# Taking both pairs of expert tiles of a step together in a fused attention and expert kernel

## The chip, the cores and the metric

The kernel runs on one core of one Trainium2 chip. The metric is the device time of one launch in microseconds; less is better. The engines are TensorE (PE; PEld is its weight load), VectorE (DVE), ScalarE (ACT), GpSimd (POOL) and SyncE (SP). SP, and here also POOL, issue DMAs in the order of their programs; a wait in such a queue holds up everything behind it.

## The reference

For 4096 token rows (two sequences of 2048, 256 features), the result is the input plus two branches over its layer norm: a linear attention of 16 heads in blocks, and an expert feed-forward of 64 routed experts (four per token, width 64) and two shared ones.

```python
xn = _layernorm(x, axis=-1)
x = x + attn(xn, slope_rate, w_qkv, w_gate, w_out, norm_w) + ffn(xn, ...)

# attn, by blocks of one head
o_inter = einsum('bhmd,bhde->bhme', qi * q_decay, kv)
qk = einsum('bhmd,bhnd->bhmn', qi, ki) * diag_decay
o_intra = einsum('bhmn,bhne->bhme', qk, vi)
kv_new = block_decay * kv + einsum('bhmd,bhme->bhde', ki * k_decay, vi)

# ffn
g = silu(einsum('nd,edf->nef', flat, wg))
u = einsum('nd,edf->nef', flat, wu)
routed = einsum('ne,nef,efd->nd', comb, g * u, wd)
```

`comb` holds the weights of the four experts that each token chose; all other entries are zero.

## The kernel before

A first phase computes the layer norm, the shared experts and the routing. A long second phase is a software pipeline of 128 steps (`NSTEP`), one for each head (16) and each group of 512 tokens (8): a step projects keys and values (`project_kv`), q and the gate for its group, and finishes the attention of the group before: key/value products (`keys_values`), scores (`scores`), attention (`attend`) and two halves of the output projection (`project_out`). Every eighth step begins a new head. The next head's weights come through the buffer `raw` in five parts, one a step (`load_head`); the last is the decay table (L389), which is issued at the end of the SP program of step s with s % 8 = 1. VectorE opens step s % 8 = 2 with `scale_out` (L891), which waits for all of them.

The routed experts ride along in steps 27 to 74 (`EXPERT0`, `EXPERT1`). The tokens' rows have been scattered to 192 tiles of 128 slots, each of which belongs to one expert; two tiles are a pair, 96 pairs in all, two pairs a step. The way of a pair q, with buffers by q % 2 unless said otherwise:

- SP loads its rows to `xs` (`load_rows`, L413). VectorE turns them by blocks of 32 into the one buffer `xz` (`turn_rows`, L1063). POOL stores `xz` to HBM and reads it back in four pieces as `xsT` (L573, L578), the transposed rows.
- SP reads the expert's number of each tile from the table `etab` into a register and issues the load of its gate and up weights (`we`, L419) and of its down weights (`wd`, L420): `load_experts`, two tiles a pair. It is called by `pair_done(q)`, behind the wait for the down matmuls of pair q, for the pair q + 2. `pair_done` then waits for the results and stores them (L437).
- TensorE multiplies gate and up (`gate_up`, L1306) into bank 7, ScalarE takes the silu (`silu_pair`, L709), VectorE the product of both (`gated`, L1068), the hidden products `hT`. TensorE multiplies them by the down weights (`down`, L1314) into banks 6 and 7, and ScalarE copies the result to `ys` (`result`, L715).

The order of each engine is written out by hand in a loop over the steps at the end of its program. In an expert step the first pair's gate/up matmuls stand before the output projection, its down matmuls behind the q projection; the scores follow, then the second pair's gate/up matmuls, `attend`, the second half of the output projection, the gate projection and the second pair's down matmuls. The table read of SP is this:

```python
e = sp.value_load(etab[0:1, bass.ds(q * 2 + j, 1)], min_val=0, max_val=E - 1)
sp.dma_start(we[r][:, j, :], at(wexp, e)).then_inc(pair_loaded[r], 16)
sp.dma_start(wd[r][j * F:(j + 1) * F, :], at(wdown, e)).then_inc(pair_loaded[r], 16)
```

SP's other work in a step: the turned keys are stored (`store_keys`, L399, behind VectorE's turning, L1029) and read back in four pieces (`load_keys`, L405), the rows of later pairs are loaded, and a part of a head's weights.

Of the kernel before, what the change touches and what calls it, by code (L numbers as in the profile page):

```python
# [8 lines left out]
I32 = mybir.dt.int32  # L9
U32 = mybir.dt.uint32  # L10
ALU = mybir.AluOpType
# [46 lines left out]
def lightning_moe(nc, x, slope, wqkv, wgate, wout, norm_w, router_w, router_bias,  # L58
# [11 lines left out]
    with top:  # L70
# [15 lines left out]
        etab = keep("etab", [1, 2 * P], I32)  # L86
# [24 lines left out]
        sg = keep("sg", [P, 2 * P])  # L111
        hT = keep("hT", [P, P])
        ys = [keep(f"ys{i}", [P, 2, D]) for i in range(2)]
        with ExitStack() as st:
            lc = sb_in(st)("lc", [P, NT, E])
        with ExitStack() as st:
            sb = sb_in(st)
            xz = sb("xz", [P, BLK, 2 * KD, TB])
            xsT = [sb(f"xsT{i}", [P, BLK, 2 * KD, TB]) for i in range(2)]
# [160 lines left out]
        xz_stored = sem("xz_stored")  # L280
# [14 lines left out]
        pair_loaded = many("pair_loaded", 2)  # L295
# [48 lines left out]
        def _(sp):  # L344
# [116 lines left out]
            for s in range(SLOTS + 1):  # L461
                q0 = 2 * (s - EXPERT0)
                experts = EXPERT0 <= s < EXPERT1
                if EXPERT0 < s <= EXPERT1:
                    pair_done(q0 - 1)
# [14 lines left out]
                if EXPERT0 - 1 <= s < EXPERT1:  # L480
                    load_rows(q0 + 5)
# [18 lines left out]
        def _(pool):  # L500
# [920 lines left out]
```

## Time and profile before

| | us |
|---|---|
| median of 3 runs | 1780.21 (1774.66 to 1787.95) |
| span of the profiled execution, first to last instruction | 1777.0 |
| TensorE busy in the span | 1718.2 (97%) |
| VectorE busy | 1308.8 (74%) |
| ScalarE busy | 718.8 (40%) |
| POOL busy | 605.1 (34%) |

The profiled execution is known by its span, which lies between the shortest and the longest of the timed runs, 3.2 us below their median. Matmul records overlap in a pipeline, so a busy TensorE is not TensorE at its peak. The time that SP spends on issuing is not counted as busy; it is read from the SP queue in order of time, and from its waits. A profile names for each idle stretch of an engine what ended it.

### The profile page before, as it was taken

How to read it: one execution, taken by the hardware profiler on the slowest of the kernel's cores; microseconds unless marked ns; L12 is line 12 of the kernel's file. 1: busy time of each engine (PE TensorE's matmuls, PEld its weight loads, DVE VectorE, ACT ScalarE, POOL GpSimd, SP SyncE). 2: the span in 40 equal slices, each digit the busy share in tenths (PEclk: the TensorE clock that was granted, in tenths of full speed). 3: DMA queues.
4: the chain of work that ended last, by engine and by line, in shares of the span. 5: the costliest groups of instructions: out<-in, count | busy, mean ns of one | idle time of the engine just before them, and what ended most of it. 6: DMA issues, size and time to landing. Idle time of an engine off the chain costs nothing.

```text
span 1777.0 us, 34485 instructions
## 1 busy us (share of the span) xinstructions
PE 1718.2 (97%) x11705; PEld 1520.5 (86%) x11705; DVE 1308.8 (74%) x2590; ACT 718.8 (40%) x1331; POOL 605.1 (34%) x826
## 2 busy tenths in 40 slices
PE   6999999999899999999999999999999999999997
PEld 5888899999788888887888888889898989899996
DVE  7888788888576666666766666668787877876666
ACT  4333343443344444444444444443334343434331
POOL 2223155655343334333333433323232424200011
PEclk9999999999999999999999999999999999999998
DMA  6666444444478888787888888844343434331234
GB/s 216 214 219 229 140 140 137 140 148 140 152 218 252 246 252 244 219 257 235 250 250 245 250 242 240 255 150 134 104 134 105 141 110 142 110 93 49 78 101 131
DMA packets 283502, 316.02 MB, mean 178 GB/s; under 512 B 37696, under 2 KB 233280, under 8 KB 283328
## 3 DMA queue, kind: packets, MB, share of 16 engines
q1 hardware_dynamic: 237120, 200.52, 36.9%
q0 software_dynamic: 33792, 88.13, 16.8%
q10 hardware_dynamic: 12416, 25.17, 3.8%
q8 instruction: 96, 1.57, 0.4%
q14 instruction: 78, 0.64, 0.1%
HBM read 169.21 MB, written 144.46 MB: 177 GB/s over the span
## 4 chain that ended last, share of the span: by engine, by line
PE 81%; DVE 7%; DMA 4%; issue 3%; SPq 3%; ACT 1%; POOL 0%; DVEq 0%; ACTq 0%
PE bank L1241 7%; PE bank L1283 6%; PE bank L1242 6%; PE bank L1243 6%; PE bank L1266 6%; PE bank L1223 6%; PE bank L1221 6%; PE bank L1222 6%; PE bank L1286 6%; PE bank L1274 5%; PE bank L1306 4%; PE bank L1314 3%; PE bank L1295 3%; PE bank L1297 3%; PE bank L1296 3%
## 5 line engine op out<-in xcount | busy, mean ns | idle before, releaser
L578 POOL DMA_DIRECT2D xsT<-rows_turned x384 | 210.7, 555 | 366.6 <-DMA rows_turned<-xz 346.8
L1241 PE MATMUL bank<-wh,xh 128*128 128x256 f32 x1024 | 293.8, 287 | 0.0
L1243 PE MATMUL bank<-wh,xl 128*128 128x256 f32 x1024 | 289.1, 282 | 0.0
L1242 PE MATMUL bank<-wl,xh 128*128 128x256 f32 x1024 | 289.0, 282 | 0.0
L674 ACT ACTIVATE kv<-bank 128x512 f32<-128x512 f32 x256 | 153.1, 598 | 229.3 <-PE bank L1243 229.3
L589 POOL DMA_INDIRECT yk<-slot_y,pos x128 | 130.5, 1020 | 270.9 <-DVE xr L995 183.6
L1283 PE MATMUL bank<-sm,kv 128*128 128x128 f32 x1024 | 201.2, 284 | 14.6 <-DVE sm L1009 14.5
L1241 PEld LDWEIGHTS bank<-wh,xh 128*128 128x128 f32 x1024 | 193.3, 189 | 19.2 <-issue 15.9
L1221 PE MATMUL bank<-xh,wh 128*128 128x512 f32 x512 | 208.9, 408 | 0.0
L1045 DVE SCALAR_TENSOR_TENSOR og<-tg,bank 128x512 f32<-128x512 f32 x128 | 88.0, 688 | 157.7 <-ACT o L700 157.7
L1223 PE MATMUL bank<-xh,wl 128*128 128x512 f32 x512 | 202.4, 395 | 0.0
L1029 DVE STREAM_TRANSPOSE kz<-kv 128x512 f32<-128x512 f32 x127 | 90.1, 710 | 151.8 <-issue 139.1
L1222 PE MATMUL bank<-xl,wh 128*128 128x512 f32 x512 | 201.8, 394 | 0.0
L1242 PEld LDWEIGHTS bank<-wl,xh 128*128 128x128 f32 x1024 | 192.6, 188 | 3.1
L1243 PEld LDWEIGHTS bank<-wh,xl 128*128 128x128 f32 x1024 | 192.9, 188 | 0.0
L1286 PE MATMUL bank<-qp,state 128*128 128x128 f32 x960 | 187.9, 278 | 0.0
L1283 PEld LDWEIGHTS bank<-sm,kv 128*128 128x128 f32 x1024 | 159.5, 194 | 30.1 <-DVE sm L1009 20.6
L681 ACT ACTIVATE qT<-bank 128x512 f32<-128x512 f32 x128 | 76.5, 597 | 234.1 <-PE bank L1223 208.5
L1058 DVE TENSOR_TENSOR acc<-acc,bank 128x512 f32<-128x512 f32 x240 | 163.6, 682 | 4.3 <-PE bank L1297 2.7
L1023 DVE SCALAR_TENSOR_TENSOR state<-state,hc,bank 128x128 f32<-128x128 f32 x448 | 152.1, 339 | 15.0 <-PE bank L1274 2.4
L700 ACT ACTIVATE o<-bank 128x512 f32<-128x512 f32 x128 | 76.7, 599 | 188.7 <-PE bank L1286 187.6
L1266 PEld LDWEIGHTS bank<-qT,kT 128*128 128x128 f32 x1024 | 129.4, 192 | 27.0 <-issue 21.6
(165 smaller groups left out, 3699.0 us busy)
## 6 DMA issues: line engine op xcount, KB each, us to landing
keys_turned<-kz SPq DMA_DIRECT2D x127, 256.0 KB, 2.9
kT_by_group<-keys_turned SPq DMA_DIRECT2D x508, 64.0 KB
slot_x<-zeros ACTq DMA_DIRECT2D x8, 3072.0 KB, 9.9
we<-wexp_in SPq DMA_DIRECT2D x192, 128.0 KB, 2.8
xs<-slot_x SPq DMA_DIRECT2D x96, 256.0 KB, 4.3
rows_turned<-xz POOLq DMA_DIRECT2D x96, 256.0 KB, 3.9
xsT<-rows_turned POOLq DMA_DIRECT2D x384, 64.0 KB, 3.2
slot_y<-ys SPq DMA_DIRECT2D x96, 256.0 KB, 2.8
```

Of the source, the lines that this page charges most:

```text
L578: pool.dma_start(xsT[q % 2][b * TB:(b + 1) * TB, :, :, :].rearrange("p a k j -> p a (k j)"), xz_back[q % 2, b]).then_inc(xsT_loaded[q % 2] ...
L674: act.activation(kv[i % 2][:, 2 * half:2 * half + 2, :].rearrange("p c n -> p (c n)"), bank[half][:], ACT.Silu).then_inc((k_silu, v_silu)[ ...
L1058: dve.tensor_tensor(a, a, bank[5][:], ALU.add).then_inc(acc_added, 1)
L1221: pe.matmul(dst, lh, rh, start=(k == 0), stop=False)
L1222: pe.matmul(dst, lh, rl, start=False, stop=False)
L1223: mm = pe.matmul(dst, ll, rh, start=False, stop=(k == KD - 1))
L1241: pe.matmul(dst, lh, rh, start=(k == 0), stop=False)
L1242: pe.matmul(dst, lh, rl, start=False, stop=False)
L1243: mm = pe.matmul(dst, ll, rh, start=False, stop=(k == KD - 1))
L1266: mm = pe.matmul(bank[2][:, ch[c]], kT[:, c, :, :].rearrange("p a j -> p (a j)"), qT[:, ch[c]], start=True, stop=True)
L1283: mm = pe.matmul(bank[4][:, ch[c]], kv[j % 2][:, c, HD:2 * HD], sm[:, ch[c]], start=True, stop=empty)
L1286: mm = pe.matmul(bank[4][:, ch[c]], state[j % 2][:, c, :], qp[j % 2][:, ch[c]], start=False, stop=True)
```

## The change

Both pairs of a step (2u and 2u + 1, a quad u) are taken together. TensorE runs the gate/up matmuls of both pairs one behind the other into all 512 columns of bank 7, where the first pair's stood, and the down matmuls of both behind the q projection. There is one silu of 512 columns, two products of twice the size (written back over `sg`, and `hT` is gone), and two result copies of 512 columns. The scores come before the q projection in every step. There are two `xz` buffers, and VectorE turns the rows of both pairs of the next step at the head of the step. SP loads gate/up weights of the next quad behind the wait for this quad's gate/up matmuls, and down weights behind the wait for its down matmuls, with a function for each; both read the expert's number from the table.

On SP, from the result store of a pair to the next, with `etab` the table, `we` the gate/up weights and `wd` the down weights; before, in the middle of an expert step:

```order
L437 DMA slot_y<-ys 128x2x256
L399 DMA keys_turned<-kz 128x512
L413 DMA xs<-slot_x 128x2x256
L418 TENSOR_LOAD etab
L418 ISA x2
L419 ISA
L419 DMA we<-wexp_in 128x256
L420 ISA
L420 DMA wd<-wdown_in 64x256
```

Now, at the last gate/up load and the first down load of a step:

```order
L420 TENSOR_LOAD etab
L420 ISA x2
L421 ISA
L421 DMA we<-wexp_in 128x256
L405 DMA kT_by_group<-keys_turned 32x4x128 x4
L428 TENSOR_LOAD etab
L428 ISA x2
L429 ISA
L429 DMA wd<-wdown_in 64x256
```

Where one table read served two loads, each load now has one of its own, and the four reads and loads of the down weights stand behind the key loads.

On TensorE, in an expert step from the end of the q projection on (`kT` and `qT` are of the scores, `sm` of `attend`); before:

```order
L1223 MATMUL bank<-xh,wl 128x512
L1314 MATMUL bank<-wd,hT 128x256 x2
L1266 MATMUL bank<-qT,kT 128x128 x4
L1306 MATMUL bank<-xsT,we 128x128 x4
L1283 MATMUL bank<-sm,kv 128x128
```

Now, from the scores on:

```order
L1277 MATMUL bank<-qT,kT 128x128 x4
L1232 MATMUL bank<-xh,wh 128x512
L1233 MATMUL bank<-xl,wh 128x512
L1234 MATMUL bank<-xh,wl 128x512
L1232 MATMUL bank<-xh,wh 128x512
L1233 MATMUL bank<-xl,wh 128x512
L1234 MATMUL bank<-xh,wl 128x512
L1329 MATMUL bank<-wd,sg 128x256 x4
L1294 MATMUL bank<-sm,kv 128x128
```

The scores moved ahead of the q projection, the second gate/up run went to the first one, and the one down run is twice as long.

The core of the diff:

```diff
...
                     sp.wait_ge(xz_ready, q - 1)
                 sp.dma_start(xs[q % 2][:], slot_x_pair[q]).then_inc(pair_rows_loaded[q % 2], 16)
 
-            def load_experts(q):
+            def load_gate_up(q):
+                if q >= NPAIR:
+                    return
                 r = q % 2
                 for j in range(2):
                     e = sp.value_load(etab[0:1, bass.ds(q * 2 + j, 1)], min_val=0, max_val=E - 1)
-                    sp.dma_start(we[r][:, j, :], at(wexp, e)).then_inc(pair_loaded[r], 16)
-                    sp.dma_start(wd[r][j * F:(j + 1) * F, :], at(wdown, e)).then_inc(pair_loaded[r], 16)
+                    sp.dma_start(we[r][:, j, :], at(wexp, e)).then_inc(we_loaded[r], 16)
+
+            def load_down(q):
+                if q >= NPAIR:
+                    return
+                r = q % 2
+                for j in range(2):
+                    e = sp.value_load(etab[0:1, bass.ds(q * 2 + j, 1)], min_val=0, max_val=E - 1)
+                    sp.dma_start(wd[r][j * F:(j + 1) * F, :], at(wdown, e)).then_inc(wd_loaded[r], 16)
 
             def first_pairs():
                 sp.wait_ge(routed, 1)
                 sp.wait_ge(wgt_ready, 1)
                 for q in range(2):
-                    load_experts(q)
+                    load_gate_up(q)
+                    load_down(q)
                 for r in range(CH):
                     sp.wait_ge(scattered[r], 16 * TOPK * NT // CH)
                 for q in range(2):
                     load_rows(q)
 
-            def pair_done(q):
-                sp.wait_ge(y_mm, q + 1)
-                if q + 2 < NPAIR:
-                    load_experts(q + 2)
-                sp.wait_ge(ys_ready, q + 1)
-                sp.dma_start(slot_y_pair[q], ys[q % 2][:]).then_inc(y_stored[q % 2], 16)
+            def next_gate_up(u):
+                sp.wait_ge(gu_mm, u + 1)
+                for r in range(2):
+                    load_gate_up(2 * u + 2 + r)
+
+            def quad_done(u):
+                sp.wait_ge(y_mm, u + 1)
+                for r in range(2):
+                    load_down(2 * u + 2 + r)
+                sp.wait_ge(ys_ready, u + 1)
+                for r in range(2):
+                    sp.dma_start(slot_y_pair[2 * u + r], ys[:, r, :, :]).then_inc(y_stored[r], 16)
 
             def load_part(t):
                 sp.wait_ge(part2_stored[t % 2], 16 * (t // 2))
...
                     store_part(COMBINE.index(s))
                 if EXPERT0 - 1 <= s < EXPERT1:
                     load_rows(q0 + 4)
+                    load_rows(q0 + 5)
                 if experts:
-                    pair_done(q0)
+                    next_gate_up(s - EXPERT0)
                 if 1 <= s < NSTEP:
                     load_keys(s)
                 if s == EXPERT0 - 2:
                     first_pairs()
-                if EXPERT0 - 1 <= s < EXPERT1:
-                    load_rows(q0 + 5)
+                if experts:
+                    quad_done(s - EXPERT0)
                 if s == EXPERT1:
                     for r in range(2):
                         sp.wait_ge(y_stored[r], 16 * NPAIR // 2)
...
                         pool.indirect_dma_start(out=slot_x, out_offset=bass.IndirectOffsetOnAxis(pos[:, q * CH + r, k:k + 1], 0),
                                                 in_=xs[r // 2][:, r % 2, :], in_offset=None).then_inc(scattered[r], 16)
 
-            for q in range(NPAIR):
-                pool.wait_ge(xz_ready, q + 1)
-                pool.wait_ge(xsT_loaded[q % 2], 16 * BLK * (q // 2))
-                pool.dma_start(xz_dram[q % 2], xz[:].rearrange("p b k j -> p b (k j)")).then_inc(xz_stored, 16)
-                pool.wait_ge(xz_stored, 16 * (q + 1))
-                if q >= 2:
-                    pool.wait_ge(gu_mm, q - 1)
-                for b in range(BLK):
-                    pool.dma_start(xsT[q % 2][b * TB:(b + 1) * TB, :, :, :].rearrange("p a k j -> p a (k j)"),
-                                   xz_back[q % 2, b]).then_inc(xsT_loaded[q % 2], 16)
+            for u in range(NPAIR // 2):
+                for r in range(2):
+                    pool.wait_ge(xz_ready, 2 * u + r + 1)
+                    pool.wait_ge(xsT_loaded[r], 16 * BLK * u)
+                    pool.dma_start(xz_dram[r], xz[r][:].rearrange("p b k j -> p b (k j)")).then_inc(xz_stored[r], 16)
+                if u > 0:
+                    pool.wait_ge(gu_mm, u)
+                for r in range(2):
+                    pool.wait_ge(xz_stored[r], 16 * (u + 1))
+                    for b in range(BLK):
+                        pool.dma_start(xsT[r][b * TB:(b + 1) * TB, :, :, :].rearrange("p a k j -> p a (k j)"),
+                                       xz_back[r, b]).then_inc(xsT_loaded[r], 16)
             for r in range(2):
                 pool.wait_ge(y_stored[r], 16 * NPAIR // 2)
             for t in range(NT):
...
                 act.wait_ge(out_mm, KD * j)
                 act.copy(ogh[:], og[:]).then_inc(ogh_ready, 1)
 
-            def silu_pair(q):
-                act.wait_ge(gu_mm, q + 1)
-                act.activation(sg[F:2 * F, :], bank[7][0:F, 0:2 * P], ACT.Silu).then_inc(sg_ready, 1)
-
-            def result(q):
-                act.wait_ge(y_mm, q + 1)
-                act.wait_ge(y_stored[q % 2], 16 * (q // 2))
+            def silu_quad(u):
+                act.wait_ge(gu_mm, u + 1)
+                act.activation(sg[F:2 * F, :, :, :].rearrange("p r j n -> p (r j n)"), bank[7][0:F, :],
+                               ACT.Silu).then_inc(sg_ready, 1)
+
+            def result(u):
+                act.wait_ge(y_mm, u + 1)
+                for r in range(2):
+                    act.wait_ge(y_stored[r], 16 * u)
                 for j in range(2):
-                    ins = act.copy(ys[q % 2][:, j, :], bank[6 + j][:, 0:D])
+                    ins = act.copy(ys[:, :, j, :], bank[6 + j][:].rearrange("p (r d) -> p r d", r=2))
                 ins.then_inc(ys_ready, 1)
 
             for s in range(NSTEP + 1):
                 experts = EXPERT0 <= s < EXPERT1
-                q0 = 2 * (s - EXPERT0)
                 projects, attends = s < NSTEP, 1 <= s
                 if projects:
                     silu_kv(s, 0)
                     silu_kv(s, 1)
-                if attends and not experts:
+                if attends:
                     copy_kT(s - 1)
                 if experts:
-                    silu_pair(q0)
+                    silu_quad(s - EXPERT0)
                 if s % NSB == 3 and s // NSB + 1 < NH:
                     if s < NSB:
                         first_phase_stored(act)
...
 
             def turn_rows(q):
                 dve.wait_ge(pair_rows_loaded[q % 2], 16 * (q // 2 + 1))
-                dve.wait_ge(xz_stored, 16 * q)
-                dve.transpose(xz[:], xs[q % 2][:].rearrange("p t (k b i) -> p b (t k) i", b=BLK, i=TB)).then_inc(xz_ready, 1)
-
-            def gated(q):
-                dve.wait_ge(sg_ready, q + 1)
+                dve.wait_ge(xz_stored[q % 2], 16 * (q // 2))
+                dve.transpose(xz[q % 2][:], xs[q % 2][:].rearrange("p t (k b i) -> p b (t k) i", b=BLK, i=TB)).then_inc(xz_ready, 1)
+
+            def gated(u):
+                dve.wait_ge(sg_ready, u + 1)
+                up = bank[7][F:2 * F, :].rearrange("p (r j n) -> p r j n", r=2, j=2)
                 for j in range(2):
-                    dve.tensor_tensor(hT[j * F:(j + 1) * F, :], sg[F:2 * F, j * P:(j + 1) * P],
-                                      bank[7][F:2 * F, j * P:(j + 1) * P], ALU.mult).then_inc(hT_ready, 1)
+                    dve.tensor_tensor(sg[j * F:(j + 1) * F, :, j, :], sg[F:2 * F, :, j, :], up[:, :, j, :],
+                                      ALU.mult).then_inc(hT_ready, 1)
 
             def mean_squares(b):
                 dve.wait_ge(rms_mm, b + 1)
...
                 if attends:
                     update_state(s - 1)
                 if experts:
-                    gated(q0)
-                if attends and not experts:
+                    if projects:
+                        decay_keys(s)
+                    gated(s - EXPERT0)
+                if attends:
                     decay_scores(s - 1)
-                if projects:
+                if projects and not experts:
                     decay_keys(s)
-                if EXPERT0 <= s + 1 < EXPERT1:
-                    turn_rows(q0 + 3)
                 if delivers:
                     add_out(s - 2, 0)
-                if experts:
-                    decay_scores(s - 1)
                 if projects:
                     decay_queries(s)
                 if s > FIRST_OUT + 2:
                     last_sum(s - FIRST_OUT - 3)
-                if experts:
-                    gated(q0 + 1)
                 if attends:
                     gate_o(s - 1)
                 if delivers:
...
                 pe.matmul(bank[5][:], lh, ogl[:], start=False, stop=False)
                 pe.matmul(bank[5][:], ll, ogh[:], start=False, stop=True).then_inc(out_mm, 1)
 
-            def gate_up(q):
+            def gate_up(u):
                 pe.wait_ge(routed, 1)
-                pe.wait_ge(pair_loaded[q % 2], 64 * (q // 2 + 1))
-                pe.wait_ge(xsT_loaded[q % 2], 16 * BLK * (q // 2 + 1))
-                pe.wait_ge(ys_ready, q)
-                for j in range(2):
-                    for k in range(KD):
-                        mm = pe.matmul(bank[7][:, j * P:(j + 1) * P], we[q % 2][:, j, k * P:(k + 1) * P],
-                                       xsT[q % 2][:, :, j * KD + k, :], start=(k == 0), stop=(k == KD - 1))
+                pe.wait_ge(ys_ready, u)
+                for r in range(2):
+                    pe.wait_ge(we_loaded[r], 32 * (u + 1))
+                    pe.wait_ge(xsT_loaded[r], 16 * BLK * (u + 1))
+                    for j in range(2):
+                        for k in range(KD):
+                            mm = pe.matmul(bank[7][:, (2 * r + j) * P:(2 * r + j + 1) * P], we[r][:, j, k * P:(k + 1) * P],
+                                           xsT[r][:, :, j * KD + k, :], start=(k == 0), stop=(k == KD - 1))
                 mm.then_inc(gu_mm, 1)
 
-            def down(q):
-                pe.wait_ge(hT_ready, 2 * (q + 1))
-                for j in range(2):
-                    ps = slice(j * F, (j + 1) * F)
-                    mm = pe.matmul(bank[6 + j][:, 0:D], hT[ps, :], wd[q % 2][ps, :], start=True, stop=True)
+            def down(u):
+                pe.wait_ge(hT_ready, 2 * (u + 1))
+                for r in range(2):
+                    pe.wait_ge(wd_loaded[r], 32 * (u + 1))
+                for r in range(2):
+                    for j in range(2):
+                        ps = slice(j * F, (j + 1) * F)
+                        mm = pe.matmul(bank[6 + j][:, r * D:(r + 1) * D], sg[ps, r, j, :], wd[r][ps, :], start=True, stop=True)
                 mm.then_inc(y_mm, 1)
 
             def total_counts():
...
```

## Rows read from the trace of the kernel before

**Rows 1.** The page's part 1: busy time, share of the span, instructions.

```profile
PE 1718.2 (97%) x11705; PEld 1520.5 (86%) x11705; DVE 1308.8 (74%) x2590; ACT 718.8 (40%) x1331; POOL 605.1 (34%) x826
```

**Rows 2.** Windows, steps 27 to 74, score matmuls (L1266) alone: busy (x records).

```profile
489.00:1178.00 689.00, 56.51 (x384) 47.27 (x384) 1.00 0.81 242
```

**Rows 3.** Same windows: us; PE, PEld, DVE, ACT, POOL busy; clock, DMA, GB/s.

```profile
489.00:1178.00 689.00, 678.89 (x4656) 577.66 (x4655) 463.25 (x924) 308.69 (x636) 259.84 (x473) 1.00 0.81 242
```

**Rows 4.** Longest of TensorE's waits in that stage: total us, times, longest.

```profile
PE bank L1314 <- DVE hT L1068: 9.5, 5, 3.0
```

**Rows 5.** Waits of the SP queue in that stage: total us, times, longest.

```profile
SPq L418 <- PE bank L1314: 45.6, 39, 2.2
SPq L399 <- DVE kz L1029: 12.4, 8, 7.8
SPq L413 <- DVE xz L1063: 4.8, 12, 0.8
SPq L436 <- ACT ys L715: 2.9, 1, 2.9
```

**Rows 6.** The SP queue in order of time, step 34: start us, us issuing.

```profile
589.50 0.36 SPq L419 DMA_DIRECT2D we<-wexp_in  x1
590.04 0.48 SPq L420 DMA_DIRECT2D wd<-wdown_in  x1
591.33 0.35 SPq L419 DMA_DIRECT2D we<-wexp_in  x1
...
597.03 0.49 SPq L420 DMA_DIRECT2D wd<-wdown_in  x1
598.97 0.36 SPq L419 DMA_DIRECT2D we<-wexp_in  x1
```

**Rows 7.** The SP queue in order of time, step 42.

```profile
702.55 0.47 SPq L389 DMA_DIRECT2D raw<-decay_tables  x1
...
709.00 0.33 SPq L399 DMA_DIRECT2D keys_turned<-kz  x1
```

**Rows 8.** VectorE in order of time, opening of step 42; idle before in brackets.

```profile
708.00 0.35 DVE L891 TENSOR_SCALAR wos<-raw 128x256 f32<-128x256 f32 x1 [5.57 <-DMA raw<-decay_tables]
708.26 0.70 DVE L1029 STREAM_TRANSPOSE kz<-kv 128x512 f32<-128x512 f32 x1
```

**Rows 9.** TensorE in order of time, first down run of step 32.

```profile
565.01 0.39 PE L1222 MATMUL bank<-xl,wh 128*128 128x512 f32 x1
565.24 0.40 PE L1223 MATMUL bank<-xh,wl 128*128 128x512 f32 x1
565.57 0.70 PE L1314 MATMUL bank<-wd,hT 64*128 64x256 f32 x4
566.20 1.16 PE L1266 MATMUL bank<-qT,kT 128*128 128x128 f32 x8
567.20 1.06 PE L1306 MATMUL bank<-xsT,we 128*128 128x128 f32 x8
568.14 0.49 PE L1283 MATMUL bank<-sm,kv 128*128 128x128 f32 x2
```

**Rows 10.** Source line 418, the table read: duration ns min/median/max.

```profile
L418 SPq TENSOR_LOAD <-etab x192: 262/273/1059, 467.7 to 1166.0; - x192
L418 SPq FUSED_REGOPS  x192: 152/156/177, 468.2 to 1166.2; - x192
L418 SPq SEQ_ASSERT  x192: 18/18/33, 468.4 to 1166.5; - x192
```

**Rows 11.** Line 389, the decay-table load: who waited (us, times); landing.

```profile
  DVE wos L891: 32.3, 12
DMA to landing us min/median/max: 2.2/3.1/5.4
```

**Rows 12.** Windows around VectorE's wait in step 42; columns as in rows 3.

```profile
705.00:710.00 5.00, 3.02 (x18) 2.28 (x16) 1.90 (x5) 1.00 (x2) 1.94 (x4) 1.00 0.74 244
710.00:715.00 5.00, 3.96 (x19) 3.48 (x20) 3.77 (x8) 1.24 (x3) 0.79 (x2) 0.66 0.72 222
```

More of the change, by code:

```diff
@@ L85, in lightning_moe @@
         wgt = keep("wgt", [P, NT, TOPK])
-        etab = keep("etab", [1, 2 * P], I32)
+        etab = keep("etab", [1, SLOT_TILES], I32)
         raw = keep("raw", [P, WC + D + 1 + TAB])
@@ L110, in lightning_moe @@
         wd = [keep(f"wd{i}", [P, D]) for i in range(2)]
-        sg = keep("sg", [P, 2 * P])
-        hT = keep("hT", [P, P])
-        ys = [keep(f"ys{i}", [P, 2, D]) for i in range(2)]
+        sg = keep("sg", [P, 2, 2, P])
+        ys = keep("ys", [P, 2, 2, D])
         with ExitStack() as st:
@@ L117, in lightning_moe @@
             sb = sb_in(st)
-            xz = sb("xz", [P, BLK, 2 * KD, TB])
+            xz = [sb(f"xz{i}", [P, BLK, 2 * KD, TB]) for i in range(2)]
             xsT = [sb(f"xsT{i}", [P, BLK, 2 * KD, TB]) for i in range(2)]
@@ L279, in lightning_moe @@
         xz_ready = sem("xz_ready")
-        xz_stored = sem("xz_stored")
         gu_mm = sem("gu_mm")
@@ L294, in lightning_moe @@
         scattered = many("scattered", CH)
-        pair_loaded = many("pair_loaded", 2)
+        we_loaded = many("we_loaded", 2)
+        wd_loaded = many("wd_loaded", 2)
+        xz_stored = many("xz_stored", 2)
         pair_rows_loaded = many("pair_rows_loaded", 2)
@@ L463, in _ @@
                 experts = EXPERT0 <= s < EXPERT1
-                if EXPERT0 < s <= EXPERT1:
-                    pair_done(q0 - 1)
                 if s > FIRST_OUT + 3:
@@ L737, in _ @@
                     act.activation(pk[:], pk[:], ACT.Exp).then_inc(pk_exp, 1)
-                if experts:
-                    copy_kT(s - 1)
-                    result(q0)
                 if projects:
@@ L743, in _ @@
                 if experts:
-                    silu_pair(q0 + 1)
+                    result(s - EXPERT0)
                 if attends:
@@ L749, in _ @@
                     tanh_g(s)
-                if experts:
-                    result(q0 + 1)
         @block.vector
@@ L974, in routing @@
                     dve.wait_ge(etab_mm, 1)
-                    dve.tensor_copy(etab[:], bank[6][0:1, 0:2 * P]).then_inc(routed, 1)
+                    dve.tensor_copy(etab[:], bank[6][0:1, 0:SLOT_TILES]).then_inc(routed, 1)
             def next_weights(s):
@@ L1094, in _ @@
                     turn_rows(q0 + 2)
+                    turn_rows(q0 + 3)
                 if 0 < s:
@@ L1108, in _ @@
                 if experts:
-                    gated(q0)
-                if attends and not experts:
+                    if projects:
+                        decay_keys(s)
+                    gated(s - EXPERT0)
+                if attends:
                     decay_scores(s - 1)
-                if projects:
+                if projects and not experts:
                     decay_keys(s)
-                if EXPERT0 <= s + 1 < EXPERT1:
-                    turn_rows(q0 + 3)
                 if delivers:
                     add_out(s - 2, 0)
-                if experts:
-                    decay_scores(s - 1)
                 if projects:
@@ L1123, in _ @@
                     last_sum(s - FIRST_OUT - 3)
-                if experts:
-                    gated(q0 + 1)
                 if attends:
@@ L1328, in squares @@
             def squares(b):
-                pe.wait_ge(ys_ready, NPAIR)
+                pe.wait_ge(ys_ready, NPAIR // 2)
                 pe.wait_ge(ssq_added, FIRST_OUT + b + 1)
@@ L1348, in _ @@
                 experts = EXPERT0 <= s < EXPERT1
-                q0 = 2 * (s - EXPERT0)
                 projects, attends, delivers = s < NSTEP, 1 <= s <= NSTEP, 2 <= s <= NSTEP + 1
@@ L1362, in _ @@
                 if experts:
-                    gate_up(q0)
+                    gate_up(s - EXPERT0)
                 if delivers:
                     project_out(s - 2, 0)
-                if attends and not experts:
+                if attends:
                     scores(s - 1)
@@ L1370, in _ @@
                 if experts:
-                    down(q0)
-                    scores(s - 1)
-                    gate_up(q0 + 1)
+                    down(s - EXPERT0)
                 if attends:
@@ L1381, in _ @@
                     turn_keys(0)
-                if experts:
-                    down(q0 + 1)
                 if FIRST_OUT + 2 <= s < SLOTS - 1:
```

## The prediction

> **What bounds the kernel now.** I read the page first, then the expert stage by windows, then the waits of TensorE and of the SP queue there, then the SP queue in order of time. The page says TensorE: busy 97% of the span [rows 1]. The expert stage is steps 27 to 74: the eight score records of a step come 384 times between 489 and 1178 us, so 48 steps take 689 us, 14.35 us each [rows 2]. TensorE is busy 678.9 us of these [rows 3]; the one wait of it there that counts is before the down matmuls, 9.5 us in five cases [rows 4]. So every step is TensorE's, and a change that leaves its matmuls as they are can win little: its small gaps and those 9.5 us.
>
> The engine that the page does not list as busy is the one to look at. SP issues DMAs in order. In the same 689 us it waited for others 65.7 us (45.6 + 12.4 + 4.8 + 2.9) [rows 5]; the other 623 us it spent issuing, 13.0 us of each 14.35 us step. The queue in order of time shows it: loads stand behind loads, a few tenths of a microsecond apart [rows 6]. SP is nearly full already, and it already runs late: the decay-table load of a head, which its program puts at the end of step 41, is issued at 702.55 us, when VectorE has already opened step 42 and stands 5.57 us until the table lands; the next key store, which comes after VectorE's turning, stands at 709.00 [rows 7, 8].
>
> **The change, part by part.**
> *TensorE.* Records stay the same in number and shape; only seams go. Going into a down run costs 0.10 us (565.24 to 565.57 against 0.23 from matmul to matmul), coming out 0.11 (566.20 to 567.20 for eight records that elsewhere come every 0.11, so 0.89) [rows 9]. One of two seams a step goes: 0.21. The attend matmuls start 0.05 us late behind the second gate/up run (567.20 + 0.89 = 568.09 against 568.14), because the masked scores have only just come; after the change the q projection and both downs lie between. Together 0.26 us a step, 12.5 us in 48. If the 9.5 us of waits went too, TensorE would need 689 - 22 = 667 us, 13.9 a step.
>
> *ScalarE and VectorE.* The same elements in fewer instructions, with slack: the hidden products stand ahead of the masked scores, and the output, score and q projection matmuls lie between gate/up and down. I cost them at nothing; the cover is gone only where VectorE starts late (below). Two row turnings at the head of step 26 instead of one, both behind the first row loads, delay that step by one turning and one load issue: 0.7 + 0.5, and I take 1.5 us.
>
> *SP.* This is the term that decides. Weights are now fetched by two functions, and each reads the expert's number from the table by itself: four table reads a step become eight, with no DMA fewer. In the 47 steps that still load, 188 reads are added. One read is three SP instructions: medians 273 + 156 + 18 ns, 0.45 us without what lies between them [rows 10]. From the queue: after a gate/up load its down load follows in 0.18 us (589.86 to 590.04, no read between); with a read between, the next load follows in 0.81 (590.52 to 591.33) or 1.45 (597.52 to 598.97) [rows 6]. Less 0.18 that is 0.63 and 1.27. So 0.45 from below, 1.27 from above; I take 0.65, by the first of the two and by the median of 273 against a longest of 1059 ns. 188 x 0.65 = 122 us.
>
> SP then has 623 + 122 = 745 us of issuing for the stage, 15.5 us a step, where TensorE asks for 13.9. Its old waits vanish, and TensorE waits for it: first for the down weights, which are issued behind the wait for the down matmuls, the key loads and four more reads. The load that is meant to be a step ahead arrives when its matmul is due.
>
> *Head steps.* Six times (34, 42, ..., 74) VectorE opens a step by waiting for the decay table, issued last by SP in the step before. Behind that load SP waits for the key store, which waits for VectorE's scaling and turning: landing 3.1 us (2.2 to 5.4) [rows 11], scaling 0.26, turning 0.70 [rows 8], less the issue's own 0.47: SP stands 3.6 us with nothing to do, 22 us in six steps. TensorE stands longer there than SP, since VectorE has the state, the keys and the hidden products to catch up with before a down can run; but SP goes on issuing meanwhile, and uses up that lead in the steps behind. So only SP's own loss counts in the sum.
>
> Sum: 623 + 122 + 22 = 767 us instead of 689, +78, and 1.5 in step 26: +79.5. On the span of 1777.0 us that is 1856.5. The runs have a median of 1780.2, 3.2 above this span, so 1860 us.
>
> Here the Trainium skill speaks against the change as well: "DMA: Bandwidth & Descriptors", section "Latency and other measured facts", puts a table read at some 600 ns at least. The trace differs: 273 ns at the median, 262 the shortest [rows 10]. By the page's figure a read with its two followers would be an estimated 0.9 us, 188 of them 169 us, and the result 1907 us; by the trace it is the sum above.
>
> **The rivals.**
> *TensorE stays the bound (faster).* Place: the SP queue in the expert steps. SP has 667 - 623 = 44 us of room at TensorE's new pace, so it decides at 44/188 = 0.23 us a read: below, the seams and waits are saved and the span is 1777 - 22 = 1755, a measured 1758 us. For it: SP does wait 45.6 us for down matmuls now, and key and row loads come earlier in the new order. Against it: the shortest read alone is 0.262 us [rows 10]. 6%; and 3% for something within 1%, where a read costs about 0.3 us.
>
> *SP full, but cheap.* A read costs 0.45 us, 85 us, and the head steps lose no more than the 12.4 us for which SP stands at the key store now: 623 + 85 + 12 = 720, +31 and 1.5, 1812 us measured. For it: many reads have no long pause. Against: the gaps of 0.63 and 1.27. 19%.
>
> *Head steps and clock worse.* The granted clock was 0.66 in the five microseconds after the VectorE wait of step 42, in which TensorE had stood 3.0 us at the longest [rows 4], against 1.00 before [rows 12]: part of it at 1.2 instead of 2.4 GHz, 0.34 x 5 = 1.7 us lost. With six stalls longer than that, 10 us; with tables landing in 5.4 us, six times 5.9 instead of 3.6 us, 14 us more; with 0.8 us a read, 28 more: 1860 + 52 = 1912 us. The Trainium skill ("TensorE: Matmul & The Clock Gate", section "HAM oscillation — how this bites in real kernels") tells of such half-rate returns after idle waits; by that rule each head step pays, and the 0.66 here agrees. Against it: where SP is the bound, slow matmuls hide behind it. 10%.
>
> That the transfers themselves bind is no rival of weight: the DMA engines are busy 0.81 of the stage [rows 3], 11.6 us of work a step, below any step discussed, and the bytes stay.
>
> **How the numbers follow.** Forecast 1860 us, 62%. Its own range comes from 0.55 to 0.75 us a read and 12 to 36 us for the heads: 1831 to 1893. The range of 80% takes in the cheap rival down to 1812 and stops short of the dear one at 1905. Faster by over 1% (which is about what a measurement of this kernel tells from no change) 0.06, within it 0.03, slower 0.91.
>
> **What would show it.** In the profile of the changed kernel: SP's named waits in the stage fall from 65.7 us to some 25, nearly all for the key store; TensorE waits before the down matmuls for down-weight loads in most expert steps and for the hidden products in six; steps of 15 to 16 us, the six of a new head longer by 4 us or more; the decay table's wait of VectorE grows from 32.3 us [rows 11] to over 60. Outside the stage nothing moves. It is wrong if SP still waits for the down matmuls in most steps, or if the stage takes less than 700 us.

## The result: 1874 us, 5% slower

| | before | after |
|---|---|---|
| median, us | 1781.65 (1774.66 to 1787.95, 4 runs) | 1874.04 (1867.00 to 1875.61, 4 runs) |
| ratio, 95% interval | 1 | 1.0529 (1.0496 to 1.0561) |
| span of the profiled execution | 1777.0 | 1873.9 |
| expert stage, steps 27 to 74 | 689.2 | 785.9 |
| in it: SP's named waits | 65.7 | 40.3 |
| in it: the rest of SP's time | 623.5 | 745.6 |
| step 26 | 17.31 | 19.93 |

The stage runs from the first key-projection matmul of step 27 to that of step 75. The two rows of SP sum to it by definition: "the rest" is the stage less the waits that the profile names, which I call issuing; an unnamed stall would be counted in it. The stage grew by 96.7 us: 122.1 more issuing, 25.4 less waiting. That SP's time is what sets the stage's length does not follow from this sum; the experiments have to show it. Step 26 grew by 2.6; what lies ahead of it came out 1.9 shorter and what lies behind the stage 0.5, so little else moved. The kernel before has one run more here than in the table ahead of the prediction.

The page of the kernel after: its part 1 (to be held against [rows 1]), the granted clock over the span in 40 slices, and the shares of the chain that ended last:

```profile
PE 1719.0 (92%) x11705; PEld 1541.7 (82%) x11705; DVE 1283.0 (68%) x2494; ACT 694.8 (37%) x1187; POOL 603.6 (32%) x826
...
PEclk9999999999999998998998998999999999999998
...
PE 48%; SPq 32%; issue 9%; DVE 7%; DMA 3%; ACT 1%; DVEq 0%; ACTq 0%
```

TensorE has the same records and the same busy time, 1719.0 us, but 92% of the span instead of 97%. A third of the chain is SP's queue, which had 3% of it before; the clock falls below 9 in slices of the stage. The same shares of the kernel before:

```profile
PE 81%; DVE 7%; DMA 4%; issue 3%; SPq 3%; ACT 1%; POOL 0%; DVEq 0%; ACTq 0%
```

Windows over the stage, all engines (columns as in [rows 3]):

```profile
489.00:1275.00 786.00, 681.27 (x4658) 599.96 (x4657) 437.20 (x826) 284.90 (x492) 257.46 (x470) 0.95 0.71 212
```

TensorE is busy less than the stage is long, and part of that time at a lower clock, 0.95 against 1.00. The DMA share fell from 0.81 to 0.71: the transfers have become sparser.

TensorE's waits in the stage, longest first (total us, times, longest), for [rows 4]:

```profile
PE bank L1329 <- DVE sg L1082: 48.4, 6, 8.9
PE bank L1329 <- DMA wd<-wdown_in: 43.5, 28, 2.4
PE bank L1277 <- issue: 10.0, 10, 2.5
```

Two waits ahead of the down matmuls stand where the 9.5 us stood: six times for the hidden products `sg`, up to 8.9 us, and 28 times for the down weights. The third row is ahead of the scores: each of its ten waits ends within 0.1 us of ScalarE's copy of the keys, which had itself waited for SP's key loads. The waits of SP, for [rows 5]:

```profile
SPq L399 <- DVE kz L1042: 36.6, 11, 7.9
SPq L451 <- ACT ys L734: 2.1, 1, 2.1
SPq L403 <- DMA keys_turned<-kz: 1.6, 1, 1.6
```

The 45.6 us for the down matmuls are gone: SP never again comes early enough for that wait to show. What it has left is the key store. The SP queue in order of time around step 42 (start, us from the first issue to the last one's end), for [rows 6, 7]:

```profile
722.29 3.70 SPq L421 DMA_DIRECT2D we<-wexp_in  x4
726.09 1.79 SPq L405 DMA_DIRECT2D kT_by_group<-keys_turned  x4
728.65 4.24 SPq L429 DMA_DIRECT2D wd<-wdown_in  x4
732.93 1.10 SPq L453 DMA_DIRECT2D slot_y<-ys  x2
734.07 0.58 SPq L389 DMA_DIRECT2D raw<-decay_tables  x1
739.70 0.34 SPq L399 DMA_DIRECT2D keys_turned<-kz  x1
740.08 0.98 SPq L413 DMA_DIRECT2D xs<-slot_x  x2
741.83 3.67 SPq L421 DMA_DIRECT2D we<-wexp_in  x4
```

Loads stand behind loads; the pauses of 0.8 us ahead of a run of weight loads hold its first table read. The four `we` loads take 3.70 us and the four `wd` loads 4.24, with the reads in between. Then comes the one hole: the decay table goes out at 734.07 and the key store at 739.70. VectorE in the same stretch, for [rows 8]:

```profile
725.98 0.68 DVE L1018 TENSOR_TENSOR ssq<-ssq,o 128x512 f32<-128x512 f32 x1
726.58 1.29 DVE L1076 STREAM_TRANSPOSE xz<-xs 128x512 f32<-128x512 f32 x2
738.70 0.35 DVE L904 TENSOR_SCALAR wos<-raw 128x256 f32<-128x256 f32 x1 [10.82 <-DMA raw<-decay_tables]
738.97 0.70 DVE L1042 STREAM_TRANSPOSE kz<-kv 128x512 f32<-128x512 f32 x1
...
741.48 0.88 DVE L1082 TENSOR_TENSOR sg<-sg,bank 64x256 f32<-64x256 f32 x2
```

It stands 10.82 us until the table lands at 738.70, scales it, turns the keys, and only then the key store can go; the product `sg`, which the down matmuls need, is finished 3.7 us after the landing. The table load's line in the stage (duration of the issue in ns, first and last start; then who waited for it: us, times), for [rows 11]:

```profile
L389 SPq DMA_DIRECT2D raw<-decay_tables x6: 503/540/582, 603.9 to 1261.4; - x6
...
  DVE wos L904: 64.5, 6
```

The six loads of the kernel before in its stage: who waited, and how long a load took to land (min/median/max):

```profile
  DVE wos L891: 25.0, 6
...
DMA to landing us min/median/max: 3.1/4.0/5.4
```

There are six waits of over 10 us on average, 64.5 us, where these six steps had 25.0 before. (The 32.3 of [rows 11] are of the whole run; the kernel after has 71.1 by that count.)

### The profile page after: what moved, and what is told of

Its sections match the earlier page's. It is cut to its first block, busy times and chain, and to the rows that moved or that the text cites. A ratio compares the mean times of both kernels' runs of the same rounds, so it can differ in the third digit from the quotient of the medians.

```text
span 1873.9 us, 34725 instructions
## 1 busy us (share of the span) xinstructions
PE 1719.0 (92%) x11705; PEld 1541.7 (82%) x11705; DVE 1283.0 (68%) x2494; ACT 694.8 (37%) x1187; POOL 603.6 (32%) x826
## 4 chain that ended last, share of the span: by engine, by line
PE 48%; SPq 32%; issue 9%; DVE 7%; DMA 3%; ACT 1%; DVEq 0%; ACTq 0%
SPq L420 5%; SPq L429 5%; SPq L428 5%; SPq L405 5%; PE bank L1294 4%; SPq L421 4%; PE bank L1253 4%; PE bank L1252 4%; PE bank L1254 4%; PE bank L1297 4%; PE bank L1234 4%; PE bank L1232 4%; PE bank L1233 4%; PE bank L1277 3%; SPq L413 3%
## 5 line engine op out<-in xcount | busy, mean ns | idle before, releaser
L1252 PE MATMUL bank<-wh,xh 128*128 128x256 f32 x1024 | 289.8, 283 | 1.5 <-ACT tg L703 1.2
L1294 PE MATMUL bank<-sm,kv 128*128 128x128 f32 x1024 | 210.1, 294 | 16.3 <-DVE sm L1022 16.2
L1294 PEld LDWEIGHTS bank<-sm,kv 128*128 128x128 f32 x1024 | 167.7, 203 | 47.1 <-DVE sm L1022 21.6
L1297 PE MATMUL bank<-qp,state 128*128 128x128 f32 x960 | 194.3, 286 | 0.0
L589 POOL DMA_DIRECT2D rows_turned<-xz x96 | 53.7, 560 | 404.5 <-DVE xz L1076 365.0
L1297 PEld LDWEIGHTS bank<-qp,state 128*128 128x128 f32 x960 | 154.9, 203 | 0.0
```

Source lines behind the costliest of these rows:

```text
L1252: pe.matmul(dst, lh, rh, start=(k == 0), stop=False)
L1294: mm = pe.matmul(bank[4][:, ch[c]], kv[j % 2][:, c, HD:2 * HD], sm[:, ch[c]], start=True, stop=empty)
L1297: mm = pe.matmul(bank[4][:, ch[c]], state[j % 2][:, c, :], qp[j % 2][:, ch[c]], start=False, stop=True)
```

## The experiments

Theory A is the prediction's: the stage is as long as SP's issuing and its own waits, so table reads and the late decay table are what costs. The rivals are named in each expectation. Each ratio is to runs of the kernel before that were taken together with that kernel. The stage, and SP's time in it by the same reckoning:

| kernel | median us | ratio to before (95%) | stage | SP waits | SP issuing |
|---|---|---|---|---|---|
| after | 1874.04 | 1.0529 (1.0496 to 1.0561) | 785.9 | 40.3 | 745.6 |
| one_read | 1779.78 | 1.0003 (0.9987 to 1.0019) | 694.9 | 59.6 | 635.3 |
| before_two_reads | 1854.57 | 1.0417 (1.0390 to 1.0443) | 766.7 | 25.7 | 741.0 |
| head_early | 1846.06 | 1.0375 (1.0356 to 1.0394) | 761.9 | 10.4 | 751.5 |
| one_read_head_early | 1739.65 | 0.9780 (0.9763 to 0.9797) | 658.8 | 12.4 | 646.4 |
| stores_act | 1808.40 | 1.0176 (1.0128 to 1.0225) | 721.4 | 33.3 | 688.1 |
| before_head_early | 1757.11 | 0.9887 (0.9839 to 0.9935) | 677.2 | 45.4 | 631.8 |
| best_stores_act | 1732.05 | 0.9749 (0.9702 to 0.9796) | 651.2 | 96.6 | 554.6 |

**one_read.** The kernel after, with one table read for both loads again:

```diff
+            expert = {}
...
+                    expert[q, j] = e
                     sp.dma_start(we[r][:, j, :], at(wexp, e)).then_inc(we_loaded[r], 16)
...
-                    e = sp.value_load(etab[0:1, bass.ds(q * 2 + j, 1)], min_val=0, max_val=E - 1)
+                    e = expert.pop((q, j))
                     sp.dma_start(wd[r][j * F:(j + 1) * F, :], at(wdown, e)).then_inc(wd_loaded[r], 16)
```

> The changed kernel, but SP keeps each expert's number from the gate/up read in a register and uses it for the down load: 188 table reads fewer in the stage, order of loads and stores as in the change. Theory A (SP's issuing is the bound, and the added reads made it so): SP falls from 746 us of issuing in the stage to about 625, 13.0 us a step, under the 13.6 us that TensorE needs; the time is 1755 to 1785 us, with TensorE's waits left only at the steps of a new head. Rival B (the new order is what costs: down weights asked for too late, or transfers that collide): the reads are hidden behind the landing of the loads, and the time stays above 1850 us.

1779.78 us: A's range, far from B's. 94 us of the loss go with the second read alone. The SP queue shows it in one place (columns as above; key loads, down loads, result stores of a step):

```profile
555.06 1.80 SPq L405 DMA_DIRECT2D kT_by_group<-keys_turned  x4
557.04 2.48 SPq L432 DMA_DIRECT2D wd<-wdown_in  x4
559.56 1.14 SPq L456 DMA_DIRECT2D slot_y<-ys  x2
```

The four down loads take 2.48 us where after took 4.24, and they follow the key loads in 0.18 us (556.86 to 557.04) where after took 0.77 (727.88 to 728.65): 2.35 us for four reads, 0.59 each. TensorE's longest wait is left for the hidden products:

```profile
PE bank L1332 <- DVE sg L1085: 28.7, 6, 6.3
```

The ordinary steps are now TensorE's again, nearly all at 13.4 to 13.7 us instead of the 14.0 to 14.25 of before, but the six steps of a new head take 22.87, 20.77, 20.40, 20.85, 21.08 and 16.67. These six are 41 us above six at 13.57 (the pace shown below), where before lost 12 to its waits and heads. So the new order's gain of 26 us in 48 steps goes into the six, and a few other late steps add 2.5. The stage is left 5.7 us longer than before and step 26 2.7 longer; the rest of the program came out 7.8 shorter (why was not tried); hence no difference.

**before_two_reads.** The kernel before, with nothing changed but a second read:

```diff
                     sp.dma_start(we[r][:, j, :], at(wexp, e)).then_inc(pair_loaded[r], 16)
+                    e = sp.value_load(etab[0:1, bass.ds(q * 2 + j, 1)], min_val=0, max_val=E - 1)
                     sp.dma_start(wd[r][j * F:(j + 1) * F, :], at(wdown, e)).then_inc(pair_loaded[r], 16)
```

> The kernel before, with one change: a second table read of the same number ahead of each down load. Theory A: SP's 623 us of issuing in the stage grow by 188 x 0.65 = 122 us to 745, more than the 689 that the stage takes, and steps become SP's: 1840 to 1870 us. Rival B (it is the order of the change, not the reads): the second read goes into the 66 us of SP's waits and the rest is hidden, at most 1790 us.

1854.57: A again. In the old order too the reads make SP the bound, by (741.0 - 623.5) / 188 = 0.62 us each. Its first wait of TensorE:

```profile
PE bank L1307 <- issue: 57.2, 33, 3.3
```

stands at the gate/up matmuls. "Issue" is a late start without a releaser that the profile names; this row does not say what is late. The semaphore records do: in all 33 cases the last of the second pair's weight loads lands 0.09 us before the matmul starts. One_read gives back 91.0 of the 96.7 us of the stage, and before_two_reads adds 77.5 without the new order: together they leave no room for another main cause.

**head_early.** The kernel after, with the head's parts issued ahead of the weight loads in the expert steps:

```diff
+                if experts and s >= 5 and (s - 5) // NSB + 2 < NH and (s - 5) % NSB < 5:
+                    load_head((s - 5) // NSB + 2, (s - 5) % NSB)
                 if experts:
                     next_gate_up(s - EXPERT0)
...
-                if s >= 5 and (s - 5) // NSB + 2 < NH and (s - 5) % NSB < 5:
+                if not experts and s >= 5 and (s - 5) // NSB + 2 < NH and (s - 5) % NSB < 5:
                     load_head((s - 5) // NSB + 2, (s - 5) % NSB)
```

> The changed kernel, but in the expert steps the part of the next head's weights is issued behind the row loads, ahead of the gate/up loads, instead of last. Theory A: only SP's own idle time at the head steps is won, the 36.6 us for which it stands at the key store, as the other steps stay SP's: 1833 to 1845 us. Rival C (what TensorE stands at the head steps is lost as a whole, 48.4 us before the down matmuls and some of the low clock behind it): 1815 us or less. Rival D (the head steps are covered by SP's lead and cost nothing): 1874 us.

1846.06, a microsecond above A's range; C and D are out. A had counted all 36.6 us of key-store waits. 7.9 of them are those of step 27, and they stay:

```profile
SPq L399 <- DVE kz L1044: 8.2, 1, 8.2
```

The six head steps held 26.7 us of them, and the stage fell by 24.0: SP's named waits by 29.9, while its issuing grew by 5.9. (The medians fell by 28.0; the profiled execution of head_early is the slowest of its four.) The six stalls of TensorE for `sg` are gone, yet it now waits for the down weights more than ever:

```profile
PE bank L1331 <- DMA wd<-wdown_in: 63.7, 42, 2.8
```

That is what "SP is the bound" means: taking away the 48.4 us of TensorE's waits, and the low clock behind them, gave back about what SP itself had stood there, and no more.

**one_read_head_early.** Both edits, the head's parts early in all steps.

```diff
-                    e = sp.value_load(etab[0:1, bass.ds(q * 2 + j, 1)], min_val=0, max_val=E - 1)
+                    e = expert.pop((q, j))
...
+                if s >= 5 and (s - 5) // NSB + 2 < NH and (s - 5) % NSB < 5:
+                    load_head((s - 5) // NSB + 2, (s - 5) % NSB)
                 if experts:
                     next_gate_up(s - EXPERT0)
```

> The changed kernel with one table read for both loads and each part of the next head's weights issued behind the row loads, in all steps. Theory A: TensorE is the bound throughout; the regular expert steps of the changed kernel that wait for nothing take 13.45 to 13.7 us, 48 of them 652 us instead of 689 before, and the later head steps lose their waits of 1 to 2 us too: 1730 to 1745 us, faster than both kernels. Rival E (SP is still so full that stalls stay, or transfers collide): 1760 us or more.

1739.65, in A's range and 2.2% faster than before: with both costs taken out the new order keeps its gain. SP has almost nothing to wait for even so,

```profile
SPq L399 <- DVE kz L1045: 8.2, 4, 7.3
```

and about a dozen steps are still 0.25 to 1.1 us longer than the same steps of best_stores_act below.

**stores_act.** The kernel after, with the 96 result stores moved from SP to ScalarE's queue:

```diff
-                sp.wait_ge(ys_ready, u + 1)
-                for r in range(2):
-                    sp.dma_start(slot_y_pair[2 * u + r], ys[:, r, :, :]).then_inc(y_stored[r], 16)
...
+            def store_results(u):
+                act.wait_ge(ys_ready, u + 1)
+                for r in range(2):
+                    act.dma_start(slot_y_pair[2 * u + r], ys[:, r, :, :]).then_inc(y_stored[r], 16)
...
                     tanh_g(s)
+                if experts:
+                    store_results(s - EXPERT0)
```

> The changed kernel with all its table reads, but the two result stores of an expert step are issued by ScalarE at the end of the step, not by SP. Theory A (what binds is the sum of all that SP issues, whatever it is): two stores of 0.59 us a step leave SP, 55 us in the stage, so SP issues about 691 us there; with some 37 us at the head steps as before the time is 1812 to 1830 us. Rival F (it is the reads themselves: a read stands behind something that the stores do not touch, and the rest of SP's work is hidden): 1860 us or more.

1808.40: 4 us below A's range, and F is out. With the reads left as they are, taking other work from SP helps: its issuing fell by 57.5 us, the stage by 64.5. TensorE's two waits (`sg`, down weights):

```profile
PE bank L1333 <- DVE sg L1086: 32.7, 6, 5.9
PE bank L1333 <- DMA wd<-wdown_in: 11.7, 12, 1.8
```

The second fell from 43.5 us to 11.7; the first is the head steps' and stays for the most part.

**before_head_early.** The kernel before, with the head's parts early:

```diff
+                if s >= 5 and (s - 5) // NSB + 2 < NH and (s - 5) % NSB < 5:
+                    load_head((s - 5) // NSB + 2, (s - 5) % NSB)
                 if experts:
                     pair_done(q0)
```

> The kernel before with nothing changed but the place of the next head's parts, behind the first row load, in all steps. It tells how much of the gain of the fast version belongs to the head's parts alone. Theory A: the five waits of TensorE in the stage (9.5 us, with some low clock and start-up behind them 13 us) and the 5 us in later head steps go: 1757 to 1767 us; the 20 to 25 us between that and the fast version's 1740 us are then the seams and waits that the change itself saves on TensorE (48 x 0.5 us). Rival G (the head's place is all the gain): about 1740 us.

1757.11, in A's range; G is out. Of the 22 us that it is faster, 12.0 come in the stage and some 9.6 outside it (spans of 1755.4 and 1777.0, less the stages). TensorE has no named wait left in the stage, SP has its old one:

```profile
SPq L418 <- PE bank L1314: 31.2, 31, 2.2
```

So this is TensorE's own pace in the old order, 677.2 / 48 = 14.11 us a step.

**best_stores_act.** The fast kernel, one_read_head_early, with the stores on ScalarE as in stores_act.

> The fast version (one read, head's parts early) with the result stores issued by ScalarE as well. Theory A: SP has over 80 us of waits there and binds nothing, so taking 55 us of issuing from it wins nothing: within 4 us of the fast version. Rival H (SP's issuing still costs in the fast version): 1725 us or less.

1732.05, 7.6 us below one_read_head_early where I had expected a difference of at most 4: a miss. I had read SP's slack of the fast kernel from a window that reached past the stage; in the stage it was 12.4 us, so SP still made some steps late. The two kernels ran on different chips and the intervals of their ratios overlap, so the difference rests on the stage, 651.2 against 658.8, the same 7.6. Now every step takes 13.40 to 13.69. The windows over the stage (columns as in [rows 3]):

```profile
488.00:1140.00 652.00, 652.00 (x4665) 582.50 (x4664) 437.38 (x827) 286.26 (x493) 258.69 (x470) 1.00 0.89 255
```

TensorE is busy in all 652.00 us at the full clock. This is its pace in the new order: 651.2 / 48 = 13.57 us a step. It beats both kernels, by 2.5% and 7.6%.

## Why the prediction was right, and where it was off

*The bound.* Right: SP's queue took TensorE's place, and the second table read is the main cause (one_read, before_two_reads). The time, 1874, lies in the range; the span forecast, 1856.5, was 17.4 us short of 1873.9: 18.9 in the stage and 1.1 in step 26, less the 2.4 by which the rest came out shorter and 0.2 of rounding. The rival in which TensorE stays the bound falls: SP's waits hold none for the down matmuls any more.

*A read at 0.65 us.* Nearly right; that the term of 122 us came out at 122.1 is luck. This difference is one between two orders. With the order held, a read costs (745.6 - 635.3) / 188 = 0.59 us by after and one_read, 110 us in all, and 0.62 by before and before_two_reads. The other 12 us are not reads: one_read has as many as before and issues for 635.3 us, not 623.5. The prediction put the longer issues of the new order at nothing. The read itself has hardly changed against [rows 10]:

```profile
L428 SPq TENSOR_LOAD <-etab x192: 262/270/750, 468.5 to 1259.0; - x192
L428 SPq FUSED_REGOPS  x192: 152/152/159, 468.8 to 1259.3; - x192
L428 SPq SEQ_ASSERT  x192: 18/18/18, 469.0 to 1259.5; - x192
```

These are 0.44 us by their medians. Another 0.13 lies between them and up to the next instruction (medians of 29, 50 and 51 ns), and some loads take longer, so that their mean in the stage is 310 ns: 0.61 us a read by its records. "SP full, but cheap", which took the read at its three instructions alone, falls, and so does the estimate of 0.9 us a read.

*"Head steps": 22 us, measured 26.7.* This term was mis-sized. The mechanism is the one foretold, six waits of 4.60, 5.04, 4.30, 4.53, 5.12 and 3.12 us from the table's issue to the key store, but the landing was taken at the median of all 16 loads of the run, 3.1 us. The six loads of the stage took 4.0 at the median already before the change (the row above); with it the term is 4.0 + 0.26 + 0.70 - 0.47 = 4.5 us, 27 us in six. After the change, behind four down loads and two stores, it took 3.8 to 4.65 in five of six: 734.07 to 738.70 above. The head steps themselves took 22.8 to 26.3 us, where the others took 15.2 in the mean, but the next steps then ran at TensorE's 13.5 on SP's lead, so only SP's own loss counted, as foretold: head_early gave 24.0 of the stage back.

*"Its old waits vanish."* This step failed, for one of them: the 7.9 us before the key store of step 27 stand in both kernels. They wait for VectorE at the opening of the stage and have nothing to do with the down matmuls. They and the head term make 7.9 + 4.7 = 12.6 of the 18.9 us by which the sum, 767, fell short of 785.9; 2.0 are four small waits for the key store, 3.7 SP's two other waits, and 0.6 is issuing.

*Step 26: 1.5 us, measured 2.6.* With the head's parts early and the new order it is 17.21, against 16.17 in the old order, so 1.0 belongs to the new order (the prediction counted 0.7 + 0.5 for it); the rest comes only where the table is late.

*Seams: 0.26 us a step, measured 0.54.* Mis-sized, without consequence for the time, since SP hid it: 14.11 against 13.57 in before_head_early and best_stores_act, in which TensorE has no named wait in the stage. Taken apart, from the first record of one run of matmuls to the first of the next: the down matmuls of a step fell from 1.265 us to 1.064, the scores from 0.995 to 0.81, the key/value projection, which followed the second down run, from 2.965 to 2.87, and gate/up from 1.765 to 1.71; that is 0.20 + 0.19 + 0.09 + 0.06, and the last holds the 0.05 that the prediction put at `attend`. It priced a way in at 0.10, where the projections of q and the gate, which stand ahead of the down runs, gained 0.01. It priced the ways out at 0.11 by taking the scores at 0.89 without a down run ahead of them, where they take 0.81, and left out the key/value projection. And it held a matmul inside a run as dear as one at its ends. TensorE in order of time, step 36 (for [rows 9]):

```profile
633.07 0.28 PE L1252 MATMUL bank<-wh,xh 128*128 128x256 f32 x1
...
641.16 0.40 PE L1234 MATMUL bank<-xh,wl 128*128 128x512 f32 x1
641.49 1.13 PE L1329 MATMUL bank<-wd,sg 64*128 64x256 f32 x8
642.55 0.49 PE L1294 MATMUL bank<-sm,kv 128*128 128x128 f32 x2
...
646.55 0.28 PE L1252 MATMUL bank<-wh,xh 128*128 128x256 f32 x1
```

The way in is the same as in [rows 9], 0.33. But the eight records take 1.06 us (641.49 to 642.55) where four took 0.63: a long run is 0.20 us cheaper than two short ones. Therefore "TensorE would need 667 us" should have said 651, and the read would have had to cost under (651 - 623) / 188 = 0.15 us for the rival in which TensorE stays the bound, or 0.09 with the 635 us of one_read.

*The clock.* Each of the six head steps brought a spell at the lower level, where before step 42 alone did. Windows around step 42's wait (columns as in [rows 3], compare [rows 12]):

```profile
729.00:734.00 5.00, 4.87 (x34) 4.12 (x33) 0.00 (x0) 1.31 (x3) 2.82 (x6) 1.00 0.56 177
734.00:739.00 5.00, 0.00 (x0) 0.00 (x0) 0.30 (x2) 0.50 (x1) 1.53 (x3) 0.77 0.69 211
739.00:744.00 5.00, 1.59 (x8) 1.18 (x8) 4.80 (x12) 0.00 (x0) 0.00 (x0) 0.50 0.58 187
744.00:749.00 5.00, 5.00 (x27) 4.33 (x24) 0.87 (x2) 1.67 (x3) 0.00 (x0) 0.71 0.47 131
```

TensorE stands from 734 on, and the granted clock falls to 0.50, which is 1.2 GHz throughout, while it begins again; in the last five microseconds TensorE is busy throughout at 0.71. The rule that the prediction cited from the Trainium skill ("TensorE: Matmul & The Clock Gate", section "HAM oscillation — how this bites in real kernels"), half rate on the return from an idle wait, agrees with this 0.50. It cost nothing that shows in the sum, as the prediction's case against that rival said: without these stalls head_early won no more of the stage than SP's own 26.7 us.

*What would show it.* The down-weight waits (28 of 48 steps, "most" is just right), six waits for the hidden products, and VectorE's wait over 60 us (64.5) came. The head steps were longer by more than 4 us. The steps between them came at 15 to 16 us only in the mean (15.2): they took 13.45 to 17.57. SP's waits fell to 40.3, not to 25, by the terms above.

## What to carry to other kernels

An engine that only issues DMAs has no busy time on the page; take the length of a stage, subtract the waits that its queue names, and compare the rest with what the busy engine needs a step. Here it was 13.0 us of a step of 14.35, and a register read that looked free in the diff became a term of the sum, times the steps. A load on which an engine's first instruction of a step depends goes ahead of the step's bulk loads in the queue: that move alone was worth 1.1% in the old order and, with one read, 2.2% in the new.

## What was not expected of the hardware

- The 64-row matmuls of the down run cost less inside a run than at its ends: four records (two matmuls) in 0.63 us, eight in 1.06, so the two added matmuls cost 0.21 us each against 0.31. Matmuls of the scores behind such a run took 0.995 us, and 0.81 without it. Why was not tried.
- A table read of SP costs some 0.6 us of the queue, though the three instructions sum to 0.44 by their medians: 0.13 us lie between them in every kernel run here, and the load, 0.27 us at its median, has a mean of 0.29 to 0.40 in these stages.
- ScalarE took over 96 stores and 48 waits at no cost that shows: in best_stores_act TensorE is busy in every microsecond of the stage.
- One_read has SP issuing for 635.3 us with the same DMAs and reads as before with 623.5. The records place this with the row loads: 92 issues took 44.3 us in the stage before and 61.2 in one_read, while the other issues together came out some 5 us shorter. Why, whether by issuing two in a row or by a stall without a name, stays open.
